# Causal attention: SyncE issues the load of the next group behind the row of maxima of the third chunk, not in front of it

## The reference

```python
q, k, v = proj(Wq, bq), proj(Wk, bk), proj(Wv, bv)      # 16 heads of 16, 2048 tokens, 4 sequences
scores = einsum('bhqd,bhkd->bhqk', q, k) / sqrt(16)     # -inf where the key lies behind the query
p = softmax(scores - max(scores))
out = einsum('bhqk,bhkd->bhqd', p, v) @ Wo.T + bo
```

## Time and profile before

| | |
|---|---|
| median of 3 runs | 5074.65 us |
| the profiled execution's own time | 5057.22 us |
| its span, first to last instruction | 5055.2 us |
| mean granted TensorE clock | 0.947 of full |
| TensorE matmul / VectorE / ScalarE / GpSimd busy | 91% / 73% / 59% / 27% |
| score matmuls of `attend`, first and last start | 229.7 and 2009.0 us |

### The profile page before, as it was taken

One profiled execution on the slowest core, in us unless ns is written; L12 is line 12 of the kernel. 1 busy time (PEld: TensorE's weight loads), 2 busy tenths in 40 slices (PEclk: granted clock), 3 DMA queues, 4 the chain that ended last, 5 costly groups with the idle time before them and its releaser, 6 DMA issues. The chain is left out here.

```text
span 5055.2 us, 92061 instructions
## 1 busy us (share of the span) xinstructions
PE 4583.6 (91%) x32224; PEld 3001.1 (59%) x32224; DVE 3672.1 (73%) x7585; ACT 2988.9 (59%) x6873; POOL 1340.2 (27%) x1844
## 2 busy tenths in 40 slices
PE   8598888889888898599999999995899999999986
PEld 7433333333333333477777777774677777777766
DVE  7487777788777775677777777763777777777746
ACT  2166667777766777365656565651566666666642
POOL 3111111111111111333333333321433333333300
PEclk9789999999998999799999999997999999999998
DMA  8723332222332220100000000001000000000007
GB/s 299 206 33 41 48 46 35 36 36 35 48 49 39 35 36 18 52 14 14 14 14 14 14 14 14 14 9 64 5 14 14 14 14 14 14 14 14 14 9 269
DMA packets 175686, 214.22 MB, mean 42 GB/s; under 512 B 75836, under 2 KB 126996, under 8 KB 169108
## 3 DMA queue, kind: packets, MB, share of 16 engines
q1 hardware_dynamic: 175252, 208.56, 18.1%
HBM read 124.05 MB, written 83.89 MB: 41 GB/s over the span
## 5 line engine op out<-in xcount | busy, mean ns | idle before, releaser
L602 ACT ACTIVATE a_pt<-a_ring 128x512 f32<-128x512 f32 (+3 forms) x2560 | 1181.0, 544 | 537.4 <-PE a_ring L713 517.9
L653 DVE TENSOR_REDUCE a_mx<-a_ring 128x2 f32<-128x1024 f32 (+3 forms) x1092 | 1127.9, 1062 | 336.8 <-PE a_ring L726 197.9
L713 PE MATMUL a_ring<-a_qs,a_ks 49*128 49x512 f32 (+3 forms) x2560 | 566.4, 450 | 155.4 <-DMA a_qs<-a_ntb 106.9
L997 POOL TENSOR_TENSOR l_rn<-l_ssm,l_half 128x8 f32<-128x8 f32 x256 | 431.3, 1685 | 945.0 <-DVE l_ssm L1279 945.0
L726 PE MATMUL a_ring<-a_ks,a_qs 48*128 48x512 f32 (+3 forms) x2560 | 566.8, 439 | 86.7 <-DMA a_v_in<-v_d 52.4
L750 PE MATMUL a_ot<-a_pt,a_vt 128*32 128x512 f32 (+3 forms) x5120 | 618.8, 564 | 1.8 <-ACT a_os L608 1.3
L713 PEld LDWEIGHTS a_ring<-a_qs,a_ks 49*128 49x128 f32 x2560 | 251.4, 190 | 563.4 <-ACT a_pt L602 272.9
L1098 ACT ACTIVATE l_pr<-l_pr,l_negm 128x256 f32<-128x256 f32 (+1 forms) x1024 | 500.7, 493 | 6.5 <-DVE l_negm L1331 6.1
L576 POOL TENSOR_TENSOR a_gate<-a_gate 128x1 f32<-128x1 f32 x512 | 98.8, 193 | 1484.0 <-ACT a_pt L602 1474.0
L726 PEld LDWEIGHTS a_ring<-a_ks,a_qs 48*128 48x128 f32 x2560 | 264.4, 196 | 345.5 <-ACT a_pt L602 188.7
L1004 POOL TENSOR_TENSOR l_work<-l_work,l_rot 128x512 f32<-128x512 f32 x256 | 357.1, 1396 | 395.5 <-DVE l_work L1287 395.5
(11 more groups left out here) (173 smaller groups left out, 9065.9 us busy)
## 6 DMA issues: line engine op xcount, KB each, us to landing
qk_d<-p_parts SPq DMA_DIRECT2D x16, 2048.0 KB, 10.9
a_qs<-qk_d SPq DMA_DIRECT2D x96, 256.0 KB, 8.7
a_ks<-qk_d SPq DMA_DIRECT2D x96, 256.0 KB, 19.0
x_d<-l_dx SPq DMA_DIRECT2D x32, 512.0 KB, 2.8
l_xt<-x_d SPq DMA_DIRECT2D x24, 513.0 KB, 3.8
p_x_in<-x SPq DMA_DIRECT2D x16, 512.0 KB, 8.9
x_d<-p_xt SPq DMA_DIRECT2D x16, 512.0 KB, 5.8
v_d<-p_vt SPq DMA_DIRECT2D x16, 512.0 KB, 11.4
```

Of the source, the lines that this page charges most:

```text
L602: act.activation(pt[:, (g * STEPS + s) % NPT, 2 * piece + f, q0:CHUNK], bank("step", g, k, f)[:, q0:CHUNK], ACT.Exp).then_inc(exp_done.sem, 1)
L653: r = dve.tensor_reduce(mx[:, pr, :, t, kc], ring[:, banks[0]:banks[1] + 1, 0:w], AX.X, ALU.max)
L713: pe.matmul(bank("step", g, k, f)[:, q0:CHUNK], ks[rows, g % NSLOT, piece, kt * P:(kt + 1) * P], qs[rows, g % NSLOT, piece, c * CHUNK + q0 ...
L997: pool.tensor_tensor(out=rn[:, a * HEADS:(a + 1) * HEADS], in0=ssm[:, a * HEADS:(a + 1) * HEADS], in1=half[:, 0:HEADS], op=ALU.pow).then_i ...
```

## The change

One line of SyncE's order. `load` 1 (the load of the next group) changes places with `row_out` 2 (the third chunk's row of maxima of the current group).

```diff
@@ -541,7 +541,7 @@
                              otok[:, c % 2].rearrange("p t h d -> p (t h) d")).then_inc(o_stored[c % 2].sem, 16)
 
             def around(do):
-                do("row_out", 1); do("load", 1); do("row_out", 2); do("out", -1); do("out", 0); do("row_out", 3)
+                do("row_out", 1); do("row_out", 2); do("load", 1); do("out", -1); do("out", 0); do("row_out", 3)
                 do("row_out", 4); do("out", 1); do("out", 2)
 
             program(dict(load=load, row_out=row_out, out=out), around)
```

## The result

| | before | after |
|---|---|---|
| median, us | 5068.45 (4 runs) | 5009.27 (4 runs) |
| lowest to highest | 5050.5 to 5079.14 | 5005.57 to 5014.88 |
| profiled execution: time, span | 5057.22, 5055.2 | 5011.24, 5009.3 |

The ratio of the times is 0.9882, with a 95% interval from 0.9858 to 0.9906: 1.2% faster, by 48 to 72 us. The forecast was 42 us less (5033, from the median of 5074.65 that stood then), the range 4985 to 5070.

What follows compares the result with a forecast made beforehand. TensorE was taken as the bound, busy 91% of the span. A gain of 3.1 us in each of groups 1 to 14 (43 us), less 1.5 in group 0, made -42: from 5074.65 to 5033 us, range 4985 to 5070.

Steps and rivals of the forecast that it cites:

- The row: Third chunk's row DMAs issue in 2.44 us on an empty queue; step 24's stall of 7.6 us goes.
- The load: Starts 2.5 us behind the row's issue, takes 29.8 us; TensorE stalls anew at unit 80, 4.2 us with the median landing.
- What else is queued behind it: On SyncE, output stores and rows behind the load are held until about 649.5, some 8 us left; costed at nothing.
- The clock: Low clock (0.50) behind the new stall at unit 80 costs 4.0 us a group.
- The sign that I had given: PEclk at 0.50 for 10 us around unit 80, and groups 107 to 108 us apart.
- The sum: A group takes 107.5 us instead of 110.6: 3.1 us gained in groups 1 to 14, 1.5 lost in group 0.
- The clock holds: Rival: clock stays full in the shorter stall at unit 80; 7.1 us gained in 14 groups, 4977 us; chance 0.12.
- The new stall costs what the old did: Rival: at unit 80, load of 31.2 us and clock price of 5.2 in every group; 5070 us; chance 0.15.
- It does not do what it says: Rival: the row is late for another reason and step 24 waits on; 5075 us; chance 0.03.
- The load becomes slower: Rival: load slows beside the engines' work, unit 80 waits longer; at 35 us a load, 5111 us; chance 0.05.
- the advice of the Trainium skill: Issue a DMA early, wait late; by this alone, the exposed 4.2 us at unit 80 add 59 us: 5134.

Runs made afterwards that it cites:

- experiment 1: Kernel before, load in front, but the third chunk's row DMAs issued from ScalarE's queue instead of SyncE's: 4983.24 us, ratio 0.9851.
- experiment 3: Changed kernel with q and v (2.0 MB) of the load in front of the third chunk's row, k behind: 4906.05 us, ratio 0.9702.
- experiment 7: Changed kernel with only q (1.5 MB) of the load in front of the third chunk's row, k and v behind: 4911.42 us, ratio 0.9682.
- experiment 5: Changed kernel with the load moved two places further, behind the stores of the two outputs: 5189.92 us, ratio 1.0239.
- experiment 8: The changed kernel measured again, nothing altered: 5000.98 us, ratio 0.987 to the kernel before.
- experiment 9: Kernel before with 48 filler matmuls, alternating between both array halves, ahead of step 24's wait in groups 1 to 14: 5052.47 us, ratio 0.999.
- experiment 2: Changed kernel with the v transfer alone in front of the third chunk's row, q and k behind: 4961.31 us, ratio 0.9821.
- experiment 4: Changed kernel with 18 filler matmuls on one array half ahead of unit 0's load wait, groups 2 to 15: 5015.33 us, ratio 0.9922.
- experiment 6: Kernel before with 30 filler matmuls on one array half ahead of step 24's wait, groups 1 to 14: 5071.42 us, ratio 1.0002.
- experiment 10: Changed kernel with 24 filler matmuls on both array halves ahead of unit 0's load wait, groups 2 to 15: 5003.4 us, ratio 0.9885.

## Why the prediction was right, point by point

**The row.** Right: all 14 waits of 7.6 us at step 24 are gone, the issue takes 2.42 us. That the queue was the cause, and not the traffic, is shown by experiment 1; that the row had time to spare, by experiments 3 and 7, where 2.0 and 1.5 MB stand in front of it and it is still in time.

**The load.** Right in size: it starts 2.46 us behind the row's issue (forecast 2.5) and lands 639.6 - 609.9 = 29.7 us later (29.8). The new wait is where it was put, at unit 80: 12 times, 3.9 us each in the mean and 0.3 to 5.8 in single groups, against 14 or 15 of 3.3 to 5.6. In groups 5, 8, 11 and 14 TensorE had paused on the way (for 1.1 to 3.0 us) with the clock low behind it; it came to unit 80 late and found next to nothing to wait for, or nothing. Experiment 5 shows the mechanism from the other side.

**What else is queued behind it.** Right: the store is held for 21.27 us, and no wait of VectorE for it appears.

**The clock.** The term that was mis-sized. I took 4.0 us a group behind the new stall. From unit 80 to the next row it is 713.27 - 639.68 = 73.6 us in group 3, against 71.2 without a low clock: 2.4, and 2.0 in the mean of groups 1 to 13. I had carried 10.1 us of low clock over from the old stalls, some 9 of them behind the restart. In the shorter stall the clock mostly fell only when the stall was over, and it was back after some 7 us: 0.56 to 646.0, 0.85 in the mean of the 4 us behind. The sign that I had given, 10 us of low clock, came in groups 6 and 10 alone, and groups were 104.2 to 107.4 us apart and not 107 to 108.

**The sum.** 105.9 us a group, 107.5 forecast. The first score matmul of `attend` starts at 227.9 and the last at 1953.8, where it was 229.7 and 2009.0. So the stage gave 53.4 us, and 42 were forecast. It comes from three parts:

- The 13 periods from the row of group 1 to that of group 14 gave 4.74 us each, 61.6 in all; I had 3.1 each, 40. This is the mis-sized clock.
- Up to the row of group 1 the kernel lost 4.9 us, and I had 1.5. Group 0 got a stall of 3.04 us at its unit 80 with 6.8 us of low clock behind it. Of the loss, 2.4 us are the price of that clock, which I had put at nothing for this group without a reason.
- From the row of group 14 to the last score matmul it lost 3.3 us, where I had a gain of 3.1. Behind a pause of group 14 the clock stayed low for 23.9 us:

```profile
1797.50:1821.40 23.90, 23.73 (x129) 10.24 (x127) 12.99 (x18) 13.38 (x27) 0.55 (x2) 0.50 0.32 44
```

So the mechanism holds, and the time came as near as it did also because two smaller terms fell short on the other side: the clock of groups 1 to 13 alone would have put it 21 us off. The medians differ by 59 us. The span of the profiled executions gained only 46, since `layers`, untouched, took 12 us more in the one after (first to last matmul of one kind 2765.3 against 2753.2 us); experiment 8 gave 64 us. What lies between 53 and these is within the spread from execution to execution (5050.5 to 5079.14 before). Of the 24 us by which 5009 lies below the forecast 5033, 11 are these parts of `attend`, and 6 are the median before, which was 5074.65 when the forecast was made and is 5068.45 here.

**The rivals.** "The clock holds" fell as it was put: the clock was low for some 7 us or more around every new stall. But the miss lies on its side. "The new stall costs what the old did" fell as well: its load of 31.2 us came together with 10.2 us of low clock in groups 6 and 10, and they took 107.4 and 107.1 us, not 110. "It does not do what it says" fell with the waits at step 24. "The load becomes slower" fell: no load of the profile after took over 31.3 us. The trace agrees in part with the advice of the Trainium skill that is cited there ("DMA: Bandwidth & Descriptors", "Rules for kernel authors"), to issue a DMA early. Among the kernels whose row is in time the earlier load is the faster one, 4906.05 us in experiment 3, 5009.27 in the changed kernel, 5189.92 in experiment 5. In the kernel before, the load is all in front of the row, and the row's lateness costs more than that wins (5068.45).

## What to carry to other kernels

A small urgent transfer behind a large one on the same queue can be late until the large one is through, as the row was here; look for it as a DMA issue that takes 20 us where its like takes 2.4. Before the two are swapped, work out the time in hand of each: where both have some, split the large one around the small one, which here gave 150 us instead of the 60 of the swap. A stall of some us has a second price in the granted clock, and that price shrinks less than the stall does: here stalls of 7.6 us cost another 3.4 (experiment 9), and stalls of 3.9 us another 2.3.

## What the runs showed of the hardware that I had not expected

- TensorE paused with nothing to wait for while the load ran, here for 3 us with the DMA engines full; the trace calls it issue. In the profile before no such pause of over 0.9 us stands in `attend`.

```profile
1158.62 0.18 PEld L713 LDWEIGHTS a_ring<-a_qs,a_ks 49*128 49x128 f32 x1 [0.84 <-DVE a_mx L653]
...
1162.12 0.18 PEld L713 LDWEIGHTS a_ring<-a_qs,a_ks 49*128 49x128 f32 x1 [3.32 <-issue]
```

It came twice at 2 to 3 us in 16 groups, here and in group 14. The trace has DMA packets of the kind "instruction". At these two pauses, and at the shorter ones of groups 5 and 11 that the profile puts down to VectorE and ScalarE, one of 16 KB starts 3.2 to 3.8 us before the pause ends and takes 1.5 to 1.9 us. In group 3 such a packet starts at 629.77 during the load, and no such pause follows. So it fits a fetch that comes late behind the load, but nothing here shows that as the cause.
- A low clock can outlast its stall by far. It was 0.50 for 23.9 us in group 14, with TensorE busy for 23.73 of them (the stretch above); the same 23.9 us came once each in experiments 2, 4, 7 and 8. Group 14 took 110.2 us from row to row where its like took 105.9, and such a group of experiment 7 109.9 where its like took 99.3. What sets this length is not shown.
- The clock fell while TensorE ran matmuls of 48 rows back to back (experiment 6). With such fillers it held in some groups and fell in others (experiments 4, 9 and 10), in both forms, so what makes the difference is not settled.
- How long an issue is held does not go by the bytes in front of it. Behind six q transfers (1.5 MB) the row was out in 2.44 us, behind q and v (2.0 MB) in 9.26, and the store behind q and k alone (3.0 MB, experiment 2) in 5.67 for two, where with v among them it took 21.27 for one. In experiment 7, behind six k transfers and v (2.0 MB), two stores took 15.41. So it is v in front that makes the issue long, and not how many transfers stand there (7 with v, 12 without): with v in front the held issue ended 1.5 to 2.7 us ahead of v's landing (group 3 of before, after, experiments 3 and 7), without it 16 us ahead of the last landing. In the trace v's elements are of 256 bytes and those of q and k of 8 KB; whether their size or their number counts was not tried.
